# Next pass's rows normalised and transposed inside the recurrence scan, and the stage between passes in a new order

## The reference

```
x = x + 0.5 * ffn(layernorm(x))
x = x + attn(layernorm(x))
x = x + 0.5 * ffn(layernorm(x))
# attn, for each head of 32:
q, k, v = silu(x@Wq), silu(x@Wk), silu(x@Wv)
log_f   = log_sigmoid(x@Wf1@Wf2);  beta = 2*sigmoid(x@Wbeta);  k = l2norm(k)
# 1024 dependent steps on a 32x32 state S: decay by exp(log_f), a rank-one correction with beta,
# + k v^T;  out = q S
y = out * sigmoid(x@Wog1@Wog2);  y = y / rms(y per head) * norm_w;  result = y @ Wo
```

## Time and profile before

| | |
|---|---|
| median of 3 runs | 1867.22 us (1866.78 to 1869.74) |
| profiled execution, its own time | 1866.42 us |
| its span, first to last instruction | 1864.6 us |
| mean granted TensorE clock | 0.932 |
| TensorE matmul busy | 1593.2 us (85%) |
| VectorE, ScalarE, GpSimd busy | 1126.5, 774.5, 760.1 us |

### The profile page before, as it was taken

One profiled execution on the slowest core, in us unless ns is written; L12 is line 12 of the kernel. 1 busy time (PEld: TensorE's weight loads), 2 busy tenths in 40 slices (PEclk: granted clock), 3 DMA queues, 4 the chain that ended last, 5 costly groups with the idle time before them and its releaser, 6 DMA issues. The chain is left out here.

```text
span 1864.6 us, 69187 instructions
## 1 busy us (share of the span) xinstructions
PE 1593.2 (85%) x26524; PEld 1302.6 (70%) x26525; DVE 1126.5 (60%) x3424; ACT 774.5 (42%) x1805; POOL 760.1 (41%) x944
## 2 busy tenths in 40 slices
PE   5499999999577988788888788887885999999994
PEld 5499999999435565355654556545564999999994
DVE  7646434444357786877868778688774546444341
ACT  2143333333267334673346733467332443333331
POOL 2554422222154651646516465164651234422221
PEclk9999999999779898798987999889897999999997
DMA  9563433232300200002000020000102833332334
GB/s 300 184 187 76 88 48 48 45 51 45 74 4 7 70 22 24 4 7 70 22 23 4 7 70 23 23 4 7 47 23 83 255 78 76 75 64 47 49 48 113
DMA packets 84233, 116.23 MB, mean 62 GB/s; under 512 B 12952, under 2 KB 74464, under 8 KB 82016
## 3 DMA queue, kind: packets, MB, share of 16 engines
q1 hardware_dynamic: 56160, 74.17, 13.1%
q0 software_dynamic: 27360, 37.80, 11.5%
q10 hardware_dynamic: 608, 2.96, 0.5%
HBM read 64.87 MB, written 54.21 MB: 64 GB/s over the span
## 5 line engine op out<-in xcount | busy, mean ns | idle before, releaser
L1065 POOL DMA_INDIRECT x<-ffn_yout,ffn_place x142 | 222.6, 1568 | 531.6 <-DVE ffn_yout L997 454.6
L1003 DVE TENSOR_TENSOR ffn_inner<-ffn_inner,ffn_bank 128x512 f32<-128x512 f32 x142 | 97.6, 687 | 349.2 <-PE ffn_bank L873 346.8
L873 PE MATMUL ffn_bank<-ffn_tileT,ffn_gate_now 128*128 128x128 f32 x2272 | 280.2, 277 | 0.0
L873 PE MATMUL ffn_bank<-ffn_tileT,ffn_up_now 128*128 128x128 f32 x2272 | 277.6, 275 | 0.0
L954 ACT ACTIVATE ffn_inner<-ffn_bank 128x512 f32<-128x512 f32 x142 | 84.8, 597 | 459.0 <-PE ffn_bank L873 459.0
L883 PE MATMUL ffn_bank<-ffn_w,ffn_inner 128*128 x1136 | 268.9, 380 | 1.7 <-DVE ffn_yout L997 1.7
L873 PEld LDWEIGHTS ffn_bank<-ffn_tileT,ffn_gate_now 128*128 128x128 f32 x2272 | 268.4, 194 | 0.1
L873 PEld LDWEIGHTS ffn_bank<-ffn_tileT,ffn_up_now 128*128 128x128 f32 x2272 | 266.1, 193 | 0.0
L883 PEld LDWEIGHTS ffn_bank<-ffn_w,ffn_inner 128*128 128x128 f32 x1136 | 205.0, 190 | 24.4 <-issue 2.5
L816 ACT COPY ffn_gate_now<-ffn_w 128x1024 f32 x142 | 148.4, 1045 | 29.9 <-issue 22.3
L816 DVE COPY ffn_up_now<-ffn_w 128x1024 f32 x142 | 99.6, 702 | 55.3 <-issue 43.9
(11 more groups left out here) (574 smaller groups left out, 3179.3 us busy)
## 6 DMA issues: line engine op xcount, KB each, us to landing
ffn_w<-in_w1t_dram SPq DMA_DIRECT2D x16, 1024.0 KB, 5.6
ffn_tile<-xs SPq DMA_DIRECT2D x122, 130.0 KB, 2.1
ffn_w<-in_w2t_dram SPq DMA_DIRECT2D x16, 512.0 KB, 6.9
at_a_sb<-x SPq DMA_DIRECT2D x32, 256.0 KB, 2.8
ffn_x<-in_x_dram SPq DMA_DIRECT2D x16, 256.0 KB, 5.5
x<-ffn_x SPq DMA_DIRECT2D x16, 256.0 KB, 6.1
x<-at_a_sb SPq DMA_DIRECT2D x16, 256.0 KB, 2.1
xs<-ffn_empty SPq DMA_DIRECT2D x23, 130.0 KB, 2.9
```

The source lines that it names most:

```text
L873: t = pe.matmul(bank[:, i * P:(i + 1) * P], half_now[half][b][:, k, i * P:(i + 1) * P], rowsT[b][:, k * P:(k + 1) * P], start=(k == 0), st ...
L1003: dve.tensor_tensor(inner[b][:, :], inner[b][:, :], p_u[b][:, :], ALU.mult).then_inc(s_act, 1)
L1065: pool.indirect_dma_start(total, bass.IndirectOffsetOnAxis(ap=place[b][:, 0:1], axis=0), yout[b][:, :], None, compute_op=ALU.add).then_inc ...
```

## The change

- **The scan** (all passes but the last) also prepares the next pass. VectorE takes the statistics of two tiles in each of the steps 2 to 5. GpSimd works out mean and variance behind its inputs of step 7 and the refined root behind those of step 8 (14 operations on 128x8). ScalarE loads the table with Ln and Exp after step 5, takes the root after step 6, and from step 7 on normalises one tile a step and copies one transposed tile a step into `xT`. TensorE transposes that tile at the end of each of the steps 8 to 15, where `spin` was. ScalarE, VectorE and GpSimd now have these 16 steps written out; TensorE keeps loops, but two of them, one for steps 0 to 7 and one for 8 to 15.
- **xT** lies in the buffer `aq` (kept through the passes now) and no longer in `gt`. The inversion's part on ScalarE therefore clears `aq` after the four `value` products and not before them (`wipe`).
- **The turnover** is a function of its own, `turnover`. It starts with the low-rank numbers. Four jobs stand ahead of the gates (two of them amid the first products, two behind the output tiles), one amid the gates (between tile 4's transposes and its small matmuls), three behind them. The forget products stand between output tiles, and their logarithms run one quarter after another on ScalarE ahead of the gates. The count on TensorE stands behind the last job and two of the square sums. On VectorE, the chain of `slot` and `place` now stands ahead of the wait for the eighth job and the first two `decay`s.

```
+            def _(pe):
+                def square(j):
+                    pe.wait_ge(s_sq, j + 1)
+                    pe.wait_ge(s_ev, j + 2)
+                    pe.matmul(SQUARES[j][:, :], headsum[:, :], sqk[j][:, :], start=True, stop=True).then_inc(s_ss, 1)
...
+                def amid(i):
+                    if i == GT // 2:
+                        pe.wait_ge(s_lf, 4)
+                        job(4)
+                low(0)
+                low(1)
+                total(0)
+                total(1)
+                job(0)
+                total(2)
+                total(3)
+                pe.wait_ge(s_fgc, 2)
+                forget(0)
+                forget(1)
+                job(1)
+                output(0)
+                output(1)
+                forget(2)
+                output(2)
+                output(3)
+                forget(3)
+                for i in range(4, NT):
+                    output(i)
+                pe.wait_ge(s_lf, 2)
+                job(2)
+                pe.wait_ge(s_lf, 3)
+                job(3)
+                r.gate_tensor(pe, 0, spare=amid)
+                job(5)
+                job(6)
+                pe.wait_ge(s_ev, 1)
+                job(7)
+                square(0)
+                square(1)
+                r.count_tensor(pe, 0)
...
+                pe.wait_ge(s_kb, 4)
+                pe.wait_ge(r.s_rows, 1)
+                keyed.tensor(pe)
...
+            def _(act):
...
+                r.std_scalar(act, 0)
+                r.turn_scalar(act, 0)
+                r.choose_scalar(act, 0)
+                act.preload_act_table_set("silu_and_others")
+                act.activation(fg[2 * RANK:FG, :], fg[2 * RANK:FG, :], ACT.Tanh, scale=0.5).then_inc(s_bt, 1)
+                for j in range(8):
+                    job(j)
+                act.preload_act_table_set("natural_log_exp_and_others")
...
+            def _(dve):
...
+                    if i in (1, 3, 5):
+                        log_f(i // 2)
+                r.moments_vector(dve, 0)
+                log_f(3)
+                r.norm_vector(dve, 0, xr)
+                r.logits_vector(dve, 0)
+                r.share_vector(dve, 0)
+                r.rank_vector(dve, 0)
+                dve.wait_ge(s_bt, 1)
+                dve.tensor_scalar(fg[2 * RANK:FG, :], fg[2 * RANK:FG, :], 1.0, None, ALU.add).then_inc(s_beta, 1)
+                r.pick_vector(dve, 0)
+                r.note_vector(dve, 0)
+                r.slot_vector(dve, 0)
+                r.place_vector(dve, 0)
+                dve.wait_ge(s_zero, 1)
+                dve.wait_ge(s_lf, 4)
+                dve.wait_ge(s_ev, 8)
+                keyed.decay(dve, 0)
...
@@ scan
+            for u in range(2, UN):
+                stage(pool, u, u % 2, False)
+                if u == STAT + NT // 2 + 1:
+                    moments(pool, link)
+                if u == STAT + NT // 2 + 2:
+                    refined(pool, link)
...
-            spin(128)
+            if not turns:
+                spin(128)
+                return
+            pe.wait_ge(s_xn, u - TURN + 1)
+            pe.wait_ge(s_xt, u - TURN + 1)
+            for c in range(KCH):
+                i = pe.transpose(psum[4 + b][:, c * P:(c + 1) * P], xn[b][:, c * P:(c + 1) * P], env["ident"][:, :])
+            i.then_inc(s_tr, 1)
...
+            with pe.Fori(0, TURN // 2) as j:
+                for b in range(2):
+                    step(2 * j + b, b)
+            with pe.Fori(TURN // 2, UN // 2) as j:
+                for b in range(2):
+                    step(2 * j + b, b, True)
...
+                if u == STAT + 3:
+                    act.preload_act_table_set("natural_log_exp_and_others")
+                if u == TURN - 2:
+                    act.wait_ge(s_var, 1)
+                    act.activation(rstd, var, ACT.Ln).then_inc(s_ln, 1)
+                    act.wait_ge(s_ln, 1)
+                    act.activation(rstd, rstd, ACT.Exp, scale=-0.5).then_inc(s_rs, 1)
+                if u >= TURN:
+                    turn(u - TURN)
+                if TURN - 1 <= u < UN - 1:
+                    if u == TURN - 1:
+                        act.wait_ge(s_nm, 1)
+                    normal(u - TURN + 1)
...
+            dve.wait_ge(s_nxt, 16 * BATCH)
+            for u in range(2, UN - 2):
+                first = 2 * (u - STAT)
+                step(u, u % 2, False, range(first, first + 2) if first < NT else ())
```

More of the change, by code:

```diff
@@ L384, in gate_tensor @@
                 r.count_tensor(pe, counts)
+            if spare is not None:
+                spare(i)
         gate(GT - 1)
@@ L1229, in attn @@
                 early = ExitStack()
-                first = {"ya": sb("ya", [P, NT, DIM], at=early), "wide4": [sb(f"wide4{i}", [P, 512], at=early) for i in range(4)]}
+                first = {"ya": sb("ya", [P, NT, DIM], at=early) if s == 0 else None, "wide4": [sb(f"wide4{i}", [P, 512], at=early) for i in range(4)]}
                 early.close()
@@ L1239, in attn @@
                     keyed = decays_and_triangles(tb, sem, psum, s, env, a_top, fsum, tk, s_tk)
-                    between(nc, tb, sem, psum, s - 1 if s > 0 else None, s, env, first, routing, keyed, setup if s == 0 else None)
+                    if s == 0:
+                        between(nc, tb, sem, psum, None, s, env, first, routing, keyed, setup)
+                    else:
+                        turnover(nc, tb, sem, psum, s - 1, s, env, first, routing, keyed)
                 fetched = {n: sem(n) for n in ("pre", "nxt")}
@@ L2330, in scan @@
         ("r", "u", "d", "Rts", "Rs", "dec", "dSs", "Ss", "Us", "Os"))
-    s_stat = sem("nstat")
-    STAT = 6
+    s_stat, s_own, s_var, s_ln, s_rs, s_nm, s_xn, s_tr, s_xt = (sem("next_" + n) for n in "stat own var ln rs nm xn tr xt".split())
+    STAT, TURN = 2, UN - NT
+    free = env["tm"][:, CHAINS * PT:]
+    xn = [free[:, i * DIM:(i + 1) * DIM] for i in range(2)]
+    mean, var, rstd, dm, off = (free[:, 2 * DIM + i * NT:2 * DIM + (i + 1) * NT] for i in range(5))
     def sync(sp):
@@ L2364, in open_gpsimd, with moments, refined, link @@
         stage(pool, u, u, True)
-    def gpsimd(pool):
-        with pool.Fori(1, UN // 2) as j:
-            for b in range(2):
-                stage(pool, 2 * j + b, b, False)
+    def moments(pool, link):
+        pool.wait_ge(s_stat, NT)
+        pool.tensor_tensor(mean, stats[:, :, 1], stats[:, :, 4], ALU.add)
+        pool.tensor_tensor(dm, stats[:, :, 1], stats[:, :, 4], ALU.subtract)
+        link(pool.tensor_tensor(var, stats[:, :, 2], stats[:, :, 5], ALU.add))
+        pool.tensor_scalar(mean, mean, 0.5, None, ALU.mult)
+        pool.tensor_scalar(var, var, 1.0 / DIM, LN_EPS, ALU.mult, ALU.add)
+        link(pool.tensor_tensor(dm, dm, dm, ALU.mult))
+        link(pool.tensor_scalar(dm, dm, 0.25, None, ALU.mult))
+        pool.tensor_tensor(var, var, dm, ALU.add).then_inc(s_var, 1)
+    def refined(pool, link):
+        pool.wait_ge(s_rs, 1)
+        link(pool.tensor_tensor(dm, rstd, rstd, ALU.mult))
+        link(pool.tensor_tensor(dm, dm, var, ALU.mult))
+        link(pool.tensor_scalar(dm, dm, -0.5, 1.5, ALU.mult, ALU.add))
+        link(pool.tensor_tensor(rstd, rstd, dm, ALU.mult))
+        link(pool.tensor_tensor(off, mean, rstd, ALU.mult))
+        pool.tensor_scalar(off, off, -1.0, None, ALU.mult).then_inc(s_nm, 1)
+    def gpsimd(pool):
+        n = [0]
+        def link(ins):
+            n[0] += 1
+            ins.then_inc(s_own, 1)
+            pool.wait_ge(s_own, n[0])
+        if nxt is None:
+            with pool.Fori(1, UN // 2) as j:
+                for b in range(2):
+                    stage(pool, 2 * j + b, b, False)
+        else:
+            for u in range(2, UN):
[4 more added lines that the diff above has]
+                    refined(pool, link)
     def tensor(pe):
-        def step(u, b):
+        def step(u, b, turns=False):
             def tiles(product):
@@ L2437, in step, with normal, turn @@
                 stage(u + 2, b, False)
+        def normal(i):
+            if i >= 2:
+                act.wait_ge(s_tr, i - 1)
+            act.activation(xn[i % 2], xa[:, i, :], ACT.Identity, bias=off[:, i:i + 1], scale=rstd[:, i:i + 1]).then_inc(s_xn, 1)
+        def turn(i):
+            act.wait_ge(s_tr, i + 1)
+            act.copy(xT[:, :, i * P:(i + 1) * P], psum[4 + i % 2][:, 0:DIM].rearrange("p (k t) -> p k t", k=KCH)).then_inc(s_xt, 1)
         for b in range(2):
@@ L2441, in scalar @@
             step(b, b, True, False)
-        with act.Fori(1, UN // 2 - 1) as j:
+        if nxt is None:
+            with act.Fori(1, UN // 2 - 1) as j:
+                for b in range(2):
+                    step(2 * j + b, b, False, False)
             for b in range(2):
-                step(2 * j + b, b, False, False)
-        for b in range(2):
-            step(UN - 2 + b, b, False, True)
+                step(UN - 2 + b, b, False, True)
+        else:
+            for u in range(2, UN):
```

(10 more changed lines are left out.)

201 lines of the change are left out of this document (184 added, 17 removed).

## The result

The changed kernel takes **1879.23 us** (median of 5 executions, 1877.35 to 1880.15) against 1867.22 us (1866.78 to 1871.57): a ratio of 1.0055, 95% interval 1.0041 to 1.0070. It is 12.0 us slower. The forecast was 1865 us with a range up to 1877 us.

A forecast was written before the change was run, and what follows sets the result against it. No engine's total was taken as the bound: the scan is a ring of short waits, the turnover a chain to the first `kb`. Turnovers gain 13.5 us, scans lose 11.7 (3.9 each), so 1867.2 - 1.8 = 1865 us, range 1852 to 1877.

The forecast's parts named there:

- Turnover: Start of a turnover to first `kb`: 53.4 us against 57.9, a gain of 4.5 us each, 13.5 over three.
- Head: Turnover start to first gate: 27.0 us against 26.4, with 1.7 us for the fallen clock; output tiles end at 22.7.
- Gates: Turnover's eight gate tiles with job 4 amid them: 10.6 us, half at full clock; 8.5 if fast, 12.8 if slow.
- The slow rival: Turnover gates: clock falls to 0.50 with job 4 inside, gates 12.8 us, gain 1.5 us a turnover; 1874 us, chance 0.30.
- Behind the gates: VectorE from end of gates to `kb`: 15.4 us against 22.0, plus 0.4 for the count; waiting for roots covered.
- 0.4 us for the count: VectorE behind the gates: `slot` waits 0.4 us for TensorE's count, which stands behind three jobs and two square sums.
- Two loops on TensorE: Scan, from step 8: loading the second loop's code costs 2.5 us a scan, bounds 0 and 4.5.
- second loop free: Scan: the second loop's code loads ahead during the first, so the scan loses 1.4 us only; 1858 us, chance 0.15.
- gates stay at 2.4 GHz: Turnover gates: jobs before and amid them keep the clock full; 1858 us, with a free loop 1850; chance 0.19.
- the clock at one level throughout: Sign of error, turnover gates: forecast wrong if the granted clock stood at either level throughout, not half and half.
- The rest of the scan: Scan without the second loop's price: 1.4 us, of it statistics 0.8, ScalarE's table load 0.3 and last copy 0.3.
- Keyed part and inversion: Behind the first `kb`: keyed part moved as a whole, GpSimd slowest, 0; inversion's clearing of `aq` on ScalarE, 0.

The follow-up runs named there:

- job_behind: The changed kernel with TensorE's job 4 behind the gates and not amid them; 1872.31 us, ratio 1.0027.
- early_count: one_loop with job 4 behind the gates and the count on TensorE behind job 6, ahead of job 7 and the square sums; 1855.85 us, ratio 0.9952.
- two_loops_only: The kernel before, with TensorE running two loops of four turns instead of one of eight in three scans, same code twice; 1885.22 us, ratio 1.0098.
- tensor_written: one_loop with TensorE's 16 steps of the three scans written out, no loop; 1953.34 us, ratio 1.0464.
- one_loop: The changed kernel with TensorE's scan as one loop of eight turns, transposes in every step, unwanted results unread; 1859.02 us, ratio 0.9958.
- slots_late: early_count with VectorE's slot and place behind the first kb and first differences, not ahead of the decays; 1855.79 us, ratio 0.9949.

## Why the prediction was wrong

- **Turnover: right in sum, in part by luck.** Forecast 4.5 us each, measured 5.4, 2.6 and 5.2. The gates came out 1.6 us shorter on average than forecast and what follows them 1.3 us longer. *Head:* tiles end at 22.0, 23.4 and 23.7 us (forecast 22.7), first gate at 25.8, 27.3 and 27.5 (27.0). The 1.7 us for the clock are what separates the turnovers: it fell for 3.4 us at the start of the second and third and not in the first. *Gates:* 9.6, 9.6 and 7.9 us, forecast 10.6; the clock was low for 3.4 us, in job 4, in two turnovers and not at all in the third. So job 4 amid the gates cost 1.7 us more than at full clock in two turnovers. Moved behind them it leaves gates of 7.5 to 8.1 us, but with the clock low in 4.4 to 4.9 us of them in job_behind, and it gained nothing until the count came earlier as well (early_count). The slow rival had the clock wrong: in the changed kernel it does not stay low through the gates once jobs stand in front. *Behind the gates:* 17.1 us, forecast 15.8. VectorE did not wait for the roots or the count, as forecast, but the addition to `fg` took 1.46 us for 0.7, the two comparisons behind it (`sel`) 1.02 for 0.28 and a `pick` product 0.95 for 0.22. All lie within GpSimd's square products (759.18 to 764.04), which stood elsewhere before; that these two engines hinder each other there is argued from the overlap, not shown. The prediction's 0.4 us for the count rested on a miscount, 20 matmuls in front of it (8.6 us) where the new list has 16 (6.9 us); in the trace the count starts 7.4 us behind the gates and `slot` is reached at 10.8. Two smaller slips move nothing: the terms of the gates add up to 10.8 and not 10.6 us, and GpSimd's "free third" of a scan is over half (33.2 of 68.6 us busy).
- **Two loops on TensorE: the step that failed.** The prediction priced it at 2.5 us a scan ("less what was already loaded ahead when the first loop runs out"), with bounds 0 and 4.5. Measured in the changed kernel: 7.4, 5.9 and 4.3 us, mean 5.9; by itself, in two_loops_only, 6.3, 4.1 and 6.3, mean 5.5. The row it came from was the right one (a first turn at 4.3 us). Two things were wrong in its use. The deduction for loading ahead had no row, and no run shows any such saving: all three packets come at the entry. And the bound above: the 4.3 us were read from S of step 0 on (875.8 us), when the first of that turn's three packets (875.4, 879.3 and 882.8 us) was already under way; in the second loop all three, and the fall of the clock behind them, lie inside the steady steps. In the first scan of the changed kernel what goes with the clock is a third of the price; in two_loops_only the stalls of over 0.5 us are 3.8, 2.0 and 2.1 us of the 6.3, 4.1 and 6.3, so it is up to two thirds (third scan, clock at 0.50 for 20.5 us). 3 x (5.9 - 2.5) is 10.2 of the 14 us by which the forecast missed; 2.8 more are the other steps of the scans. The prediction also took the second loop as entered without a jump, though its own list has one in front of it (L2735). tensor_written has no jump and pays as well, so the jump is not needed for the cost.
- **The rival "second loop free"** gave 1858 us. With the second loop taken away the kernel takes 1859.02: its arithmetic held, its mechanism did not. The Trainium skill, "Runtime: NRT & Kernel Launch", section "Instruction fetch mechanics", has the crossing of a 16 KiB block mostly hidden by fetching ahead. The trace disagrees for this code of TensorE: 1.4 us a block (tensor_written), 1.8 to 2 with the second loop (5.5 and 5.9 us over three blocks).
- **The rival "gates stay at 2.4 GHz"** came about in single turnovers only: in the third of the changed kernel and the second of one_loop the clock was full throughout the gates, job 4 among them, and they took 7.9 us; in the others it was not. So one of the prediction's signs of being wrong (the clock at one level throughout) was met in one turnover of three. Without job 4 amid them the gates took 7.5 to 8.1 us in job_behind, early_count and slots_late, at a granted clock of 0.69 to 0.77 over the stretch. early_count, which has the one loop as well, stands at 1856, where that rival with a free loop gave 1850.
- **The rest of the scan.** Forecast 1.4 us. one_loop, which has all of it, is 0.9, 1.2 and 3.3 us over the kernel before, 2.2 of the last in the first two steps, where the earlier trace rows and the other traces differ by as much from execution to execution. The statistics' 0.8 us fit the 0.5 to 1.2 us of the steps 3 to 7, without being shown by themselves. For ScalarE 0.6 us were forecast, for GpSimd and the transposes nothing; together they show as some 0.2 us in the steps 8 to 15 of one_loop. In the changed kernel these steps cost up to 3.2 us (third scan), where the clock stayed low until 16.5 us behind S of step 0 (until 1135.0); in one_loop it was full again 9.0 us behind it.
- **Keyed part and inversion: nothing,** as forecast. The reason given for the first (GpSimd starts it with the first `kb`) is not the whole of it: slots_late moved that start without any gain.

## What to carry to other kernels

For code as dense as this (three packets of 16 KB for two steps of 4.1 us), a hardware loop on TensorE pays: code that the engine had not yet run cost some 1.4 to 2 us for each 16 KB, the loop's own code nothing in its later turns. When work is to be added to a part of a loop's turns, let every turn do it and throw the unwanted results away, if the engine has room, sooner than write a second body. Price an unknown by the whole of its nearest row; a deduction from it needs a row of its own.

## What the runs showed of the hardware

- Instruction packets of 16 KB for TensorE come where the code is used, also in code that runs straight on: behind S of step 0, 23 packets and 30 us more in a scan written out (tensor_written), 1 packet in a loop (one_loop). Stalls of over 0.5 us inside a run of equal matmuls end 1.2 to 1.6 us after such a packet has landed (before, after, two_loops_only, tensor_written); not every packet has a stall (15 of the 23).
- Behind stalls of 0.8 to 2.1 us the granted clock fell to 0.50 (1.2 GHz): for 13.6 us after the first of three, in the first scan of the changed kernel, and for 3.4 us after one of 0.84 us in two_loops_only; it was 0.57 on average in the scan written out.
- One TensorE job of four matmuls amid the gates ran at 0.50 in two of three turnovers (3.46 and 3.28 us, in the third 1.96), with nearly all of the gates around it at full clock.
